# Two closing stages of a two-layer attention and expert kernel: their loads put into the order of first use, the output bias loaded once, and the two float32r parts of a number made by plain conversion

## The reference

```python
# layer 0
x = x + _L0_xattn_ref(_layernorm(x), ctx_1024, ctx_1024, ...)   # 16 heads, window of 65 keys, then ctx @ o_w.T + o_b
x = x + _L0_ffn_ref(_layernorm(x), ...)                         # the recurrent cell below
# layer 1
x = x + _L1_xattn_ref(_layernorm(x), ctx_1024, ctx_1024, mask, ...)   # 16 heads, all 1601 keys, then context @ W_o.T + b_o
x = x + _L1_ffn_ref(_layernorm(x), Wg, W1, b1, W2, b2)          # 8 experts, 2 of them for each token

def _L0_ffn_ref(x, wf, uf, bf, wi, ui, bi, wc, uc, bc, wo, uo, bo, in_c):
    def step(c, xt):                       # over the batches, one after the other
        ft = sigmoid(xt @ wf.T + c @ uf.T + bf)
        it = sigmoid(xt @ wi.T + c @ ui.T + bi)
        gt = tanh(xt @ wc.T + c @ uc.T + bc)
        return ft * c + it * gt, None
    c_final, _ = lax.scan(step, c0, x)
    return tanh(x @ wo.T + c_final @ uo.T + bo)
```

## Time and profile before

| | |
|---|---|
| median of 3 runs | 4918.41 (4910.6 to 4920.52) |
| the profiled execution, its own time | 4924.39 |
| its span | 4922.6 |
| granted TensorE clock, mean over the span | 0.953 of full speed |
| PE, DVE, ACT, POOL busy | 93%, 75%, 57%, 27% |
| close_window | from 717.2 to about 1175 |
| close_full | from 3815.0 to about 4009 |

### The profile page before, as it was taken

How to read it: one execution, slowest core, us unless ns; L and a number is a source line. 1 busy time by engine, 2 the same in 40 slices (tenths; PEclk the granted TensorE clock), 3 DMA queues, 4 the chain that set the end, 5 groups by cost and what they waited for, 6 DMA issues and landing times. The chain is left out here.

```text
span 4922.6 us, 82307 instructions
## 1 busy us (share of the span) xinstructions
PE 4569.5 (93%) x28528; PEld 2726.1 (55%) x28528; DVE 3693.2 (75%) x8750; ACT 2826.7 (57%) x5187; POOL 1330.2 (27%) x940
## 2 busy tenths in 40 slices
PE   8979978996699999999999999999999657999998
PEld 4546646885244444444444444444443546988897
DVE  8978856654768888888888888888885676555554
ACT  4535542332337777777777877777777013444443
POOL 7910002222620110110111101101100223666665
PEclk9989988998879999999999999999998868999999
DMA  6666653213754333343333343332330651333332
GB/s 203 194 172 187 187 155 109 83 68 125 252 105 80 50 68 77 61 82 75 57 68 68 71 82 68 59 72 62 64 62 10 197 144 30 67 82 65 63 66 38
DMA packets 248366, 471.05 MB, mean 96 GB/s; under 512 B 56584, under 2 KB 149384, under 8 KB 247936
## 3 DMA queue, kind: packets, MB, share of 16 engines
q1 hardware_dynamic: 217872, 426.43, 35.5%
q0 software_dynamic: 26720, 38.36, 4.7%
q10 hardware_dynamic: 3360, 0.98, 0.1%
HBM read 240.15 MB, written 144.94 MB: 78 GB/s over the span
## 5 line engine op out<-in xcount | busy, mean ns | idle before, releaser
L1205 DVE TENSOR_REDUCE full_peak<-full_item 128x1 f32<-128x512 f32 (+2 forms) x3392 | 2026.3, 655 | 331.1 <-PE full_item L1267 323.1
L1181 ACT ACTIVATE full_prob<-full_score 128x512 f32<-128x512 f32 (+1 forms) x3328 | 1745.7, 601 | 396.0 <-PE full_score L1277 380.6
L1267 PE MATMUL full_item<-full_kst,full_qst 49*128 49x512 f32 (+1 forms) x4096 | 1170.0, 403 | 8.4 <-DMA full_kst<-full_high 5.6
L1277 PE MATMUL full_score<-full_qst,full_kst 51*128 51x512 f32 (+1 forms) x3328 | 1021.8, 434 | 1.2 <-ACT full_prob L1181 1.2
L1267 PEld LDWEIGHTS full_item<-full_kst,full_qst 49*128 49x128 f32 x4096 | 618.9, 188 | 602.4 <-DVE full_peak L1205 537.6
L1287 PE MATMUL full_value<-full_prob,full_vaug 128*17 128x512 f32 x6656 | 884.4, 603 | 0.6 <-ACT full_prob L1181 0.4
L1277 PEld LDWEIGHTS full_score<-full_qst,full_kst 51*128 51x128 f32 (+1 forms) x3328 | 503.5, 183 | 368.0 <-ACT full_prob L1181 297.6
L1120 POOL TENSOR_TENSOR full_low<-full_low,full_keep 128x1601 f32<-128x1601 f32 x32 | 116.0, 3625 | 1996.2 <-ACT full_low L1155 1996.2
L2509 ACT ACTIVATE moe_h<-moe_hbank,moe_b 128x384 f32<-128x384 f32 (+1 forms) x320 | 200.0, 625 | 442.9 <-PE moe_hbank L2680 403.2
L2690 PE MATMUL moe_ybank<-moe_w_both,moe_h_high 128*128 128x512 f32 x1088 | 386.7, 396 | 0.0
L2543 DVE TENSOR_TENSOR moe_h_low<-moe_h,moe_h_high 128x384 fp32r<-128x384 f32 (+1 forms) x320 | 194.6, 619 | 222.6 <-ACT moe_h_high L2499 212.1
(11 more groups left out here) (299 smaller groups left out, 6872.1 us busy)
## 6 DMA issues: line engine op xcount, KB each, us to landing
full_kst<-full_high SPq DMA_DIRECT2D x256, 200.1 KB
full_ctxT<-in_ctxT SPq DMA_DIRECT2D x16, 1601.0 KB, 8.2
full_kst<-full_low SPq DMA_DIRECT2D x128, 200.1 KB
win_qst<-scratch_q SPq DMA_DIRECT2D x384, 64.0 KB, 2.9
full_qst<-scratch_q SPq DMA_DIRECT2D x384, 64.0 KB
scratch_attn<-win_raw SPq DMA_DIRECT2D x64, 256.0 KB
scratch_q<-open_parts SPq DMA_DIRECT2D x64, 256.0 KB, 3.8
scratch_attn<-full_raw SPq DMA_DIRECT2D x64, 256.0 KB, 2.2
```

The source lines that it names most:

```text
L1181: nc.scalar.activation(prob_of(s, h, kt)[0:rows, :], score[score_bank(u)][0:rows, :], ACT.Exp, scale=SCALE).then_inc(score_read, 1)
L1205: nc.vector.tensor_reduce(peak[s.par][:, hq:hq + len(qts), c], src, AX, ALU.max).then_inc(item_read, 1)
L1267: ins = nc.tensor.matmul(ps[:, at:at + z - a], qst[s.slot][rows, h // 2, qt * P:(qt + 1) * P].bitcast(F32R), kst[s.slot][rows, h // 2, a:z ...
L1277: nc.tensor.matmul(score[score_bank(u)][0:z - a, :], kst[s.slot][rows, h // 2, a:z].bitcast(F32R), qst[s.slot][rows, h // 2, :].bitcast(F3 ...
```

## The change

In both stages SP issues the loads in another order, `bo` is one tile of [128, 256] loaded once and repeated by the access pattern of the bias addition, and the one semaphore of the constants becomes three: `wo_in`, `bo_in`, and `const_in` for `ident` and `wz`. PE begins without a wait for constants and waits for `wo` ahead of the first projection. POOL waits for `bo` alone and issues the second piece of `spread` behind the first bias addition. In close_window the second tile of sums is loaded last, and `split_weights` stands ahead of the second batch's addition in DVE's list.

The parts: ACT converts the transposed bank straight into `x_high`, DVE subtracts it from the bank, and `xT` and `x_cut` are gone. The gate weights are converted by ACT at the very start of its list, once all six have landed, and DVE subtracts. `split_state` converts and subtracts.

```diff
         @block.sync  (close_window)
             load_sums(0)
-            loads(0)
-            sp.dma_start(wo ...).then_inc(const_in, 16)
-            sp.dma_start(wz ...).then_inc(const_in, 16)
-            sp.dma_start(ident ...).then_inc(const_in, 16)
-            for i in range(QT):
-                sp.dma_start(bo[:, i, :], d["bo0"].partition_broadcast(P)).then_inc(const_in, 16)
-            loads(1)
-            load_sums(1)
+            load_attention(0)
+            sp.dma_start(wo ...).then_inc(wo_in, 16)
+            load_rows(0)
+            sp.dma_start(bo[:, :], d["bo0"].partition_broadcast(P)).then_inc(bo_in, 16)
+            sp.dma_start(ident ...).then_inc(const_in, 16)
+            load_attention(1)
+            sp.dma_start(wz ...).then_inc(const_in, 16)
+            load_rows(1)
             for k in WEIGHTS:
                 sp.dma_start(raw[k] ...).then_inc(raw_in, 16)
...
+            load_sums(1)
         @block.gpsimd  (both)
             pool.dma_start(spread[:, 0:2, :, :], d["spread"][:, 0:2]).then_inc(spread_in[0], 16)
-            pool.dma_start(spread[:, 2:8, :, :], d["spread"][:, 2:8]).then_inc(spread_in[1], 16)
-            pool.wait_ge(const_in, 16 * CONSTS)
+            pool.wait_ge(bo_in, 16)
             def add_bias(n):
-                nc.gpsimd.tensor_tensor(res ..., res ..., bo[:, :, :], ALU.add).then_inc(res_ready, 1)
+                nc.gpsimd.tensor_tensor(res ..., res ...,
+                                        bo[:, :].unsqueeze(1).broadcast_to([P, QT, D]), ALU.add).then_inc(res_ready, 1)
             add_bias(0)
+            pool.dma_start(spread[:, 2:8, :, :], d["spread"][:, 2:8]).then_inc(spread_in[1], 16)
         @block.scalar  (close_window)
-                    nc.scalar.copy(xT[n % 2][:, c, :], tbank[c][:, :]).then_inc(t_read, 1)
+                    nc.scalar.copy(x_high[n % 2][:, c, :], tbank[c][:, :]).then_inc(x_high_done, 1)
+            act.wait_ge(raw_in, 16 * len(WEIGHTS))
+            for name in WEIGHTS:
+                nc.scalar.copy(w_high[name] ..., raw[name][:, :]).then_inc(w_high_done, 1)
         @block.vector  (close_window)
             def split_x(n):
-                    nc.vector.tensor_scalar(x_cut ..., xT ..., HIGH_BITS, None, ALU.bitwise_and).then_inc(x_cut_done, 1)
-                    nc.vector.tensor_tensor(x_low ..., xT ..., x_cut[c][:, :], ALU.subtract).then_inc(x_low_done, 1)
+                    nc.vector.tensor_tensor(x_low[n % 2][:, c, :], tbank[c][:, :], x_high[n % 2][:, c, :].bitcast(F32),
+                                            ALU.subtract).then_inc(x_low_done, 1)
             def split_state(n, m):
-                nc.vector.tensor_scalar(state_cut ..., HIGH_BITS, None, ALU.bitwise_and).then_inc(state_cut_done, 1)
-                nc.vector.tensor_copy(state_high ..., state_cut[m][:, :]).then_inc(state_high_done, 1)
+                nc.vector.tensor_copy(state_high[n % 2][:, m, :], state[n % 2][:, m, :]).then_inc(state_high_done, 1)
...
                 if n >= 1:
                     next_state(n - 1, 1)
+                if n == -1:
+                    split_weights()
                 if n + 2 < BATCH:
                     add(n + 2)
...
                 if n == -1:
-                    split_weights()
                     first_state()
         @block.tensor  (close_window)
-            pe.wait_ge(const_in, 16 * CONSTS)
             spread_inverse(0)
+            pe.wait_ge(wo_in, 16)
             for n in range(-2, BATCH):
                 if n + 2 < BATCH:
                     project(n + 2)
+                if n == -1:
+                    pe.wait_ge(const_in, 16 * CONSTS)      # CONSTS = 2
         @block.sync  (close_full)
             load_sums(0)
-            loads(0)
-            wo, wz, ident, 4 x bo, bv
+            bv, wo, bo
+            loads(0)
+            ident, wz
             loads(1)
         @block.vector  (close_full)
-                for i in range(QT):
-                    nc.vector.tensor_tensor(bo[:, i, :], bo[:, i, :], obank[1][:, 1, :], ALU.add).then_inc(bias_ready, 1)
+                nc.vector.tensor_tensor(bo[:, :], bo[:, :], obank[1][:, 1, :], ALU.add).then_inc(bias_ready, 1)
         @block.tensor  (close_full)
-            pe.wait_ge(const_in, 16 * CONSTS)
+            pe.wait_ge(wo_in, 16)
...
-                pe.wait_ge(bias_ready, QT)
             spread_inverse(0)
+            if last:
+                pe.wait_ge(bias_ready, 1)
             project(0)
             spread_inverse(1)
+            pe.wait_ge(const_in, 16 * CONSTS)
```

103 lines of the change are left out of this document (41 added, 62 removed).

## The result

| | before | after |
|---|---|---|
| median, on the same chip | 4915.59 (4 runs) | 4876.55 (4873.42 to 4883.85, 4 runs) |
| ratio | | 0.9916, interval 0.9901 to 0.9931 |
| the profiled execution, its span | 4922.6 | 4882.1 |
| close_window, first load of the sums to the store of `cu`, made from the last state | 456.8 | 435.9 |
| open_full and full_attention | 2641.0 | 2642.0 |

The change makes the kernel faster by 39 us by the medians and by 41 by the ratio (its interval is 34 to 49). That range was counted from a median of 4918.41; with the fourth run the median of the kernel before is 4915.59, 2.8 lower, and this is no work of the change.

The account below looks back on a forecast made before the run. PE's own work bounds the steady part, load order and DVE's and ACT's lists the starts. 18.1 in close_window plus 13.1 in close_full make 31.2, from median 4918.4 to 4887.2; range 4878 to 4901.

Parts of the forecast that it names:

- Steady state, 0: Both stages: removing x and state masks and ACT's extra passes gains 0, as they lie beside a PE that never waits.
- Start of close_window, first part: PE starts at about 724.5, needing only the inverse and `spread`'s first 256 KB; first addition at 731.2, 11.2 earlier.
- The weights' landing, 743: Start of close_window: all six gate weights land at 743, before 746.8; conversion, subtractions and second addition are counted from there.
- The rival by which the queue stays the bound: Weights land at 746.8 as before, rows late in close_full: 23.3 won, time 4895; chance 0.2.
- the upper bound that was worked out from the landing, 21: Start of close_window: gain of 21 in place of 18.1 if the weights land at the early bound, 740.
- From the second addition to the first output product: close_window: 6.5 to the first mask as before, two subtractions 1.3, first output product at 756.6, not 774.75.
- Start of close_full, 13.1: Small loads land before the inverse is done: bias product 11.5 earlier, spreading follows at once, 13.1 us won.
- The rest of close_full, forecast as unchanged: close_full after its start: later batches keep the same pace, gain 0.
- The second piece of `spread`, cost 0: close_window: 768 KB issued behind the first bias addition near 730, needed at about 749; cost 0, covered by some 8 us.
- The bound of 740 for the weights' landing: Start of close_window: early bound on the landing, with `spread`'s second piece falling behind the weights, 3.2 us.
- The repeated bias, 2344 ns: POOL's bias addition with repeated operand, 1024 columns, takes 2344 ns as before; it matters beside close_full's centrings.
- The rival that ended slower: Repeated bias slows POOL's 14 additions beside close_full's centrings; at 6.5 us each 58 are lost, 4945; chance 0.03.

Follow-up runs that it names:

- collision taken out: Kernel before with one bias addition per stage moved ahead of POOL's root (batch 3's in close_window, batch 2's in close_full): 4918.24 against 4916.11, one execution each.
- close_window alone: Only close_window changed, close_full as in the kernel before: 4896.95 (5 runs), ratio 0.9959 against the kernel before.
- both with the order on POOL turned round in close_full: Changed kernel with POOL's bias addition ahead of the root in close_full: from batch 0 on 4864.6, ratio 0.9895; from batch 2 on 4853.17, ratio 0.9871.

## Why the prediction was right and where it was off

Two steps failed, and both carried an old collision along. In close_window it is "From the end of the addition (757.65) to the first mask (764.16) it was 6.5", taken over unchanged: it measured 4.5. In close_full it is the term of nothing for all that follows the start ("the later batches at the same pace"): the first gap fell from 10.8 to 8.1, and from the first `var_eps` to the last the stage took 2.0 less in the pair of profiles and 4.5 less in the means. In both places DVE's centring had run beside an addition of POOL at 3.40; now POOL's addition waits for its rows, and the centring runs alone at 1.38. By term:

**Steady state, 0: right.** From the first output product to the last state product it is 393.1 before and 393.4 after, and within 1.1 of the first in all thirteen kernels of the experiments.

**Start of close_window, first part: right.** First spreading 7.2 into the stage against 7.3 forecast, first addition 14.6 against 14.0.

**The weights' landing, 743: right as a place, wrong as the gate.** 25.7 into the stage against 25.8; that it fits to 0.1 is luck, as the same code also gave 23.2, 24.4 and 25.3. The rival by which the queue stays the bound (746.8, that is 29.6) is dead. But the sum counts from this landing on, and with the weights' subtraction moved out of the way the second addition ended at 31.7 in place of 32.0: PE's second projection holds it as long. The forecast had this projection at "about 746" and ready in time; in after DVE waited for it until 746.3. So the upper bound that was worked out from the landing, 21, had no ground: an earlier landing alone would have won next to nothing.

**From the second addition to the first output product: size off by 2.0.** The end of the second addition came at 32.0 against 31.6 (29.4 to 32.0 over four executions). From there to the first mask, now the first subtraction, it measured 4.5 and not 6.5, in all four. The 6.5 had a centring of 3.40 in it, with POOL's addition beside it, as the prediction's own paragraph on the repeated bias says; with the rows of the fourth batch not yet there, the centring ran alone at 1.38. Two experiments show it from both sides: the added addition of POOL put the 4.5 back to 6.1, and the kernel before with this one collision taken out has 4.5 as well. The other 0.5 run the opposite way.

**Not in the sum: the end of close_window, 1.7.** From the last state product to the store of `cu` it is 6.2 before and 4.5 after. Over the fifteen profiles this has two values, 4.5 in four and 6.1 or 6.2 in eleven, and three kernels whose close_window is that of after, line for line (close_window alone and both with the order on POOL turned round in close_full), are among the eleven. In after PE's granted clock over this end is 1.00, in before and in close_window alone it is 0.72. So it is chance of one execution and no work of the change.

**Start of close_full, 13.1: right.** Up to the first `var_eps` it took 35.3 before and 19.7 after, 15.5 less, but the means over executions of the same code are 34.3 and 21.2, 13.2 less. The terms: bias product 11.8 earlier (forecast 11.5), and 10.9 in the means; from it to the spreading 2.1 less (forecast 1.6), in every execution. The rest of the 15.5, 1.6, goes with the clock of PE: over the first two projections it was 0.60 to 0.71 in the four executions of before's code and 1.00 in after, but 0.64 to 0.67 in three others of after's code. That the change made the clock rise sooner is therefore not shown.

**The rest of close_full, forecast as unchanged: the second step that failed.** From the first `var_eps` to the last it is 149.8 before and 147.8 after, and 151.4 and 146.9 in the means. The first gap, 10.8 before and 8.1 after (means 10.8 and 7.8), is shown from both sides: with the collision taken out of the kernel before it was 7.5, with one put into after it was 10.2. The other 1.5 of the means lie in later gaps, and their cause stays open. How long such a gap is (7.5, 9.5, some 10.8, some 12) depends on the collision and on when the clock falls. In before, in the kernel with the collision taken out and in all five of after's code the last gap is 5.8, and in the other three of before's code it is 9.2 to 9.7.

**The second piece of `spread`, cost 0: right as a cost, wrong as a whole.** Nothing waited for it. But the step counted only when it is needed, not what it pushes aside while it moves: issued at the start it costs the first output product of close_window some 4 to 6 us, a collision of 2.0 among them, and close_full 4 to 7, by one execution against four and five. That gain was partly in the forecast under another name: the 11.2 of the first part assumed that sums, attention, `wo` and the first piece get the whole 243 GB/s. The bound of 740 for the weights' landing, with this piece falling behind them, had no ground: the piece moved beside the weights.

**The repeated bias, 2344 ns: right.** The rival that ended slower is dead at 2344 ns measured. It did look at the right place, the centring beside POOL's addition, but asked only what a longer addition would cost, not what a missing one would give: turned round from batch 2 on, that pair gives 29.6 in close_full (179.4 to 149.8).

**The sum.** To the 31.2 forecast the pair of profiles adds 2.9 in close_window (1.5 and 1.7, less 0.3 in the steady part), 4.5 in close_full and 2.0 in the untouched stages: 40.6, the difference of the spans. By the means it is plainer: 21.3 in place of 18.1, 13.2 in place of 13.1 and 4.5 in place of 0, less 0.2 at the end of close_full, make some 38.7, near the 39.0 of the medians. Of the 7.5 above the forecast 2.0 are the centring in close_window and 3.0 the first gap in close_full, both shown by experiments; 1.2 in close_window lie ahead of the centring, within the spread of its four executions, and 1.5 in close_full stay open. The range's low end was built from bounds on the queue and had no term for a centring that runs alone. The miss of 1.5 is smaller than the 2.8 by which the base moved: counted from 4915.59, the low end would be 4875.2 and the time inside it. That speaks for the 4 us added at each end for the spread of the runs, and not for the sum, which was short by some 8.

## What to carry to other kernels

When a stall shrinks, don't carry the chain behind it over with its old durations: go through each instruction of it and ask what lay beside it then and what will lie beside it now. An engine's list is a queue: put an instruction whose input may be late (an addition that waits for a load) behind a short one that another engine waits for, unless its input is surely there, in which case put it where the other engine has nothing to read. And a bulk load in a second queue costs those in the first while it moves; issue it when nothing urgent is in flight. Before a difference of a few us is read from two profiles, read the same stretch in other profiles of the same code.

## What the runs showed of the hardware

- Four centrings on DVE (128x256, tile and two scalars for each row, float32) take 1.38 alone. Beside a POOL addition of 128x1024 they take 3.40, which is the addition's 2.34 and most of their own 1.38 one after the other; beside an in-place one of 1.89 they take 2.95. POOL's time hardly moves (2.33 to 2.35, once 2.49). A tiny instruction is held too: `var_eps` of 128x4 took 1.56 beside an addition and 0.17 alone. The Trainium skill, "GPSIMD Engine Reference", section on specifications, says that GpSimd shares its SBUF interfaces with VectorE and contends with instructions in a 2-port mode or with two SBUF inputs. The trace agrees that they contend, and that not every instruction does. Held beside a POOL addition were the centring and `var_eps`, and the subtraction of two SBUF tiles (0.68 alone, 2.48 there, in the kernel with the late subtraction of the weights):

```profile
753.31 2.37 POOL L1493 TENSOR_TENSOR cwin_res<-cwin_res,cwin_bo 128x1024 f32<-128x1024 f32 x1 [3.28 <-DMA cwin_res<-in_x]
...
753.75 2.48 DVE L1614 TENSOR_TENSOR cwin_w_low_wf<-cwin_gate_f,cwin_w_high_wf 128x512 fp32r<-128x512 f32 x1
```

Not held were the addition and the scaling, each with one operand in a PSUM bank (0.69 for one, 1.29 for two), and the statistics (1.40). Where DVE is held it waits until POOL is done: one of the four centrings takes 2.43 and the other three 0.40 each.
- An operand repeated four times by its access pattern costs POOL nothing: 2344 ns for 128x1024, as for four copies.
- After a wait of 2.8 us PE showed a granted clock of 0.66 over the next 5 us, and after one of 1.0 it stayed at 1.00. Between the two the length alone doesn't tell: after one of 2.1 it was 0.67 over the next 5 us (the kernel with one collision taken out), and after one of 2.2 in after, at 3825.4, it stayed at 1.00.
- The end of close_window, a chain with the same code, takes 4.5 us at a granted clock of 1.00 and 6.2 at 0.72, from one execution to the next. With such two-valued pieces a single profile can't show a difference of 2 us.
- Two DMA queues with work share the rate of the moment: with both busy, SP's queue moved 259 KB in 2 us and POOL's 474; with SP's alone busy it moved 619.
